# One more identity product for each node tile in three TensorE stages of a graph network kernel

## What is computed

```
x = x + L0_gnn(layernorm(x), ...)
x = x + L0_ffn(layernorm(x)[None], gate_w, gate_b, w1, b1, w2, b2, gamma, beta)[0]   # 16 experts, 2 chosen
x = x + L1_gnn(...)                                                                  # graph attention and a selective scan
x = x + L1_ffn(...)       # h = x @ W_gat (256 x 16), a_src and a_dst from it, 4 experts
x = x + L2_gnn(...)
x = x + L2_ffn(...)       # logits = x @ gate_w (256 x 8), 1 of 8 experts
x = x + L3_gnn(...)
x = x + L3_ffn(...)       # a router of two layers: relu(x @ router_w1) @ router_w2, 6 experts
```

## Time and profile before

| | |
|---|---|
| time, three executions | 5540.38, 5551.18 and 5554.88 us, median 5551.18 |
| span of the profiled execution (with the profiler on) | 6173.2 us; what lies around the span is not in the trace |
| PE busy | 4074.4 us, 66% |
| PEld busy | 2897.1 us, 47% |
| DVE, ACT, POOL busy | 3273.6, 2796.0 and 3072.9 us |
| mean granted TensorE clock | 0.802 of full speed |

### The profile page before, as it was taken

One profiled execution on the slowest core, in us unless ns is written; L12 is line 12 of the kernel. 1 busy time (PEld: TensorE's weight loads), 2 busy tenths in 40 slices (PEclk: granted clock), 3 DMA queues, 4 the chain that ended last, 5 costly groups with the idle time before them and its releaser, 6 DMA issues. The chain is left out here.

```text
span 6173.2 us, 66416 instructions
## 1 busy us (share of the span) xinstructions
PE 4074.4 (66%) x17366; PEld 2897.1 (47%) x17366; DVE 3273.6 (53%) x7095; ACT 2796.0 (45%) x6254; POOL 3072.9 (50%) x3130
## 2 busy tenths in 40 slices
PE   7888555567837777256485776857776774555665
PEld 4555333347824445222264444835555662223465
DVE  6444355456555566699634665255556125444532
ACT  4777333322335566466343442335553213666532
POOL 3666566633446566267414552436662323666333
PEclk8999777768957887699796887967776886777888
DMA  4444533355643333355502223543333324566356
GB/s 129 150 150 148 114 90 91 90 124 180 174 115 91 94 96 95 72 167 166 135 1 61 47 43 104 179 118 95 95 95 70 118 63 129 179 181 181 81 159 203
DMA packets 442553, 721.00 MB, mean 117 GB/s; under 512 B 150695, under 2 KB 322521, under 8 KB 437660
## 3 DMA queue, kind: packets, MB, share of 16 engines
q1 hardware_dynamic: 299057, 374.14, 21.6%
q0 software_dynamic: 139600, 337.72, 20.1%
q10 hardware_dynamic: 3530, 4.89, 0.2%
HBM read 565.71 MB, written 153.73 MB: 117 GB/s over the span
## 5 line engine op out<-in xcount | busy, mean ns | idle before, releaser
L631 PE MATMUL ps<-msg,same 128*125 128x256 f32 (+1 forms) x2496 | 953.6, 524 | 671.2 <-issue 269.6
L631 PEld LDWEIGHTS ps<-msg,same 128*125 128x125 f32 x2496 | 566.1, 251 | 986.6 <-issue 574.2
L888 POOL DMA_INDIRECT msg<-d_gat,src_i x416 | 406.0, 976 | 266.9 <-PE ps L949 137.8
L253 POOL DMA_INDIRECT rec<-rec,slot_i x391 | 379.7, 971 | 304.4 <-DVE rec L431 133.6
L607 POOL DMA_INDIRECT msg<-d_lin,src_i x416 | 393.2, 945 | 275.0 <-issue 101.9
L607 POOL DMA_INDIRECT msg<-rel_rows,src_rel x416 | 399.0, 959 | 223.1 <-issue 95.4
L607 POOL DMA_INDIRECT msg<-d_gat,src_i x416 | 393.5, 946 | 226.3 <-PE ps L631 90.7
L949 PE MATMUL ps<-msg,same 128*125 128x260 f32 x832 | 300.5, 495 | 175.9 <-DVE agg_c L1111 130.9
L278 PE MATMUL ps_f<-w,hs 128*128 128x256 f32 x1568 | 383.6, 398 | 48.9 <-DVE rec L431 30.4
L278 PEld LDWEIGHTS ps_f<-w,hs 128*128 128x128 f32 x1568 | 298.8, 196 | 156.9 <-issue 61.3
L2962 PE MATMUL ps_y<-pr,ident 128*128 128x447 f32 (+1 forms) x448 | 209.3, 593 | 238.3 <-DVE pr L3044 238.3
(11 more groups left out here) (632 smaller groups left out, 9885.5 us busy)
## 6 DMA issues: line engine op xcount, KB each, us to landing
w<-in_L_ffn_packed SPq DMA_DIRECT2D x170, 514.0 KB
fil<-rec SPq DMA_DIRECT2D x104, 512.0 KB
rows<-bc_d SPq DMA_DIRECT2D x96, 447.0 KB
rel_rows<-row SPq DMA_DIRECT2D x25, 896.0 KB
got<-answered SPq DMA_DIRECT2D x30, 560.0 KB
ahead<-in_L_ffn_packed SPq DMA_DIRECT2D x8, 2052.0 KB
lo_rows<-ffn_lo_r SPq DMA_DIRECT2D x32, 500.0 KB
msg<-d_gat,src_i POOLq DMA_INDIRECT x832
```

The lines of the kernel that those rows point to most:

```text
L253: nc.gpsimd.indirect_dma_start(k.rec, bass.IndirectOffsetOnAxis(slot_i[0:some_rows, c:c + 1], 0), rec[0:some_rows, g % R, j, :], None).the ...
L631: nc.tensor.matmul(ps[:, j, 0:width], same[:, g % 2, j, :], msg[:, g % R, j, 0:width], start=True, stop=True).then_inc(mm, 1)
L888: nc.gpsimd.indirect_dma_start(msg[:, g % R, j, :], None, table, bass.IndirectOffsetOnAxis(idx[:, n:n + 1], 0)).then_inc(msg_in[g % R], 16)
```

## The change

In the fronts without a router, and in the small head, TensorE does one more product for each tile: the identity as weights, the identity as moving operand, 128 columns, into a PSUM bank `ps_w` that nothing reads. It stands between the turning of a later tile and the narrow product of tile t. The product carries no wait and no semaphore. In the small head the bank comes from `ps_t`, which goes from four banks to three there, and the wait of `turn(t)` becomes one for the copy of tile t - 3. The wide heads and the front with a router keep their instructions.

```diff
@@ front
         else:
             w_sb = s.sb("w", [128, 2, L])
+            ps_w = s.ps("ps_w", [128, 128])
...
+                def keep_streaming():
+                    nc.tensor.matmul(ps_w[:], k.ident[:], k.ident[:], start=True, stop=True)
+
...
                     else:
+                        keep_streaming()
                         logits(t)
@@ head
-        ps_t, ps = s.ps("ps_t", [128, 4, 512]), s.ps("ps", [P, 4, 512])
+        narrow = width < 128
+        TURNED = 3 if narrow else 4
+        ps_t, ps = s.ps("ps_t", [128, TURNED, 512]), s.ps("ps", [P, 4, 512])
+        if narrow:
+            ps_w = s.ps("ps_w", [128, 128])
...
-                    if t >= 4:
-                        pe.wait_ge(copied, t - 3)
-                    nc.tensor.transpose(ps_t[:, t % 4, 0:P], rows[:, t, 0:128], k.ident[0:P, 0:P])
+                    if t >= TURNED:
+                        pe.wait_ge(copied, t - TURNED + 1)
+                    nc.tensor.transpose(ps_t[:, t % TURNED, 0:P], rows[:, t, 0:128], k.ident[0:P, 0:P])
...
                 for t in range(NT):
                     if t + 1 < NT:
                         turn(t + 1)
+                    if narrow:
+                        nc.tensor.matmul(ps_w[:], k.ident[:], k.ident[:], start=True, stop=True)
                     product(t)
```

More of the change, by code:

```diff
@@ L2326, in turn @@
                     pe.wait_ge(rows_done, t + 1)
-                    if t >= 4:
-                        pe.wait_ge(copied, t - 3)
-                    nc.tensor.transpose(ps_t[:, t % 4, 0:P], rows[:, t, 0:128], k.ident[0:P, 0:P])
-                    nc.tensor.transpose(ps_t[:, t % 4, P:2 * P], rows[:, t, 128:256], k.ident[0:P, 0:P]).then_inc(turned, 1)
+                    if t >= TURNED:
+                        pe.wait_ge(copied, t - TURNED + 1)
+                    nc.tensor.transpose(ps_t[:, t % TURNED, 0:P], rows[:, t, 0:128], k.ident[0:P, 0:P])
+                    nc.tensor.transpose(ps_t[:, t % TURNED, P:2 * P], rows[:, t, 128:256], k.ident[0:P, 0:P]).then_inc(turned, 1)
                 def product(t):
@@ L2356, in copy @@
                     act.wait_ge(turned, t + 1)
-                    nc.scalar.activation(cols[:, :, t * P:(t + 1) * P], ps_t[:, t % 4, 0:2 * P].rearrange("p (c n) -> p c n", c=2), ACT.Copy).then_inc(copied, 1)
+                    nc.scalar.activation(cols[:, :, t * P:(t + 1) * P], ps_t[:, t % TURNED, 0:2 * P].rearrange("p (c n) -> p c n", c=2), ACT.Copy).then_inc(copied, 1)
                 def keep(t):
```

## The result

The changed kernel takes 5577.78 us (median of five executions, 5574.15 to 5592.81) against 5549.69 us before (five, 5535.66 to 5554.88). The ratio is 1.0062 with a 95% interval of 1.0047 to 1.0077, so the change costs 26 to 43 us. The forecast was 5583.2 us.

What follows compares the result with a forecast made beforehand. The prediction took each of the three changed stages to be bound by TensorE at half clock; 75 added products at 0.43 us gave 32 us, so 5551.2 + 32.0 = 5583.2 us, with an eight-in-ten range of 5546 to 5596.

Steps and rivals of the forecast that it cites:

- The price of the product: Three changed stages: each added product costs two weight-load steps, 0.43 us at half clock, 0.22 at full.
- The sum of 32 us: All three changed stages: 75 added products at 0.43 us each, 10.7 us a stage.
- The bound from above: Added product priced as a two-matmul product that overlaps nothing: 0.59 us each, 44 us in all.
- The bound from below: Added product priced as two steps of the narrow products: 0.37 us each, 28 us in all.
- Nothing covers it: Three changed stages: TensorE's stream has no gap and DVE and ACT wait for it, so all 32 us show.
- The clock: Three changed stages: at 340 to 380 moving columns a us the clock stays at 0.50; chance 0.70.
- the bursts of 100 columns: Two bursts of 16 float32 matmuls, 428 columns a us within a burst, stayed at 0.50; used as comparison for the clock.
- A front rises in its opening: Rival: a front's dense opening, 490 columns a us, lifts the clock; one front saves 16.5 us, 5567 us; chance 0.12.
- If all three had risen: Rival: steady streams of all three stages reach clock 1.00, saving 17.4 us together, 5534 us; chance 0.13.
- The bank: Small head: losing one `ps_t` bank adds a wait that is always met; cost nothing.
- The queues: Stores and loads issue as before; DVE's rows wait for ACT's root, not TensorE; no cost of their own.
- From one execution to the median: The 32 us from the profiled execution is carried over unscaled to the unprofiled median of 5551.18 us.

Runs made afterwards that it cites:

- e2: Changed kernel with the added product cut to 16 moving columns from 128: 5577.99 us against 5544.13 for the kernel before, ratio 1.0058.
- e3: Changed kernel with two added products a tile in place of one, one behind the other: 5550.52 us against 5544.13 for the kernel before, ratio 1.0016.
- e5: Kernel before, no added product, narrow product widened with zero weights to 64 moving columns: 5549.28 us against 5544.02, ratio 1.0004.
- e9: Changed kernel with two added products a tile, the second between the two narrow products: 5589.49 us against 5540.27 for the kernel before, ratio 1.0088.
- e8: Kernel before plus float32 identity transposes ahead of the first turn (28 in fronts; 24 and 10 in small head), no product a tile: 5543.8 us, one execution.
- e6: Changed kernel plus identity products in the idle opening (14 in fronts; 12 and 5 in small head): 5523.02 us against 5544.02 for the kernel before, ratio 0.9953.
- e1: Kernel before with only the small head's turned-tile banks cut from four to three, no added products: 5553.8 us against 5544.1, one execution.
- e7: Kernel before plus identity products in the idle opening (14 in fronts; 12 and 5 in small head), none a tile: 5542.24 us against 5544.02, ratio 0.9991.

## Why the prediction was right, and where it was not

**The price of the product.** Two steps of 0.215 us, 0.43 us a tile, were forecast from the router front's rows; the changed front shows 0.43 and a tile of 1.587 us for 1.58. The sum of 32 us compares with 32.5 in the stretches. The bound from above, 0.59 us, was never near. The bound from below I had misread: a turn takes 0.46 us and not 0.42 (1348.16 to 1348.62), which leaves 0.35 us for two narrow steps, 26 us and not 28. What I had not said is whether the product's columns cost anything: e2 shows that they don't.

**Nothing covers it.** Right: all of it shows in the time, as the three stages are bound by TensorE at half clock.

**The clock.** The outcome was right: 0.50 in all three. The step behind it was only half right. That a stage can be busy throughout and not rise is borne out: the changed fronts are busy for 40.05 of 40.10 us and stay at half. But I compared means over a tile and leaned on the bursts of 100 columns as if they were a safe bound from above. The case was closer than I made it: with a second product the clock rises in the second front at 395 a us, 4% above the small head's 380 and below the bursts' 428. And the mean orders neither e3 against e5 nor e3 against e9. So the 0.50 was forecast with a measure that the runs don't bear out, and there was luck in it. Why the clock stays at half with one product and rises with two in a row is open.

The closing table of TensorE: Matmul & The Clock Gate, a page of the Trainium skill, advises to keep TensorE busy without a break for the full clock; this case does not agree, as the changed fronts have next to no break in 40 us and don't reach it, so the busy time that it speaks of must not be read off the profile's busy columns. Part 4 of the same page of the Trainium skill says that transposes don't count as other matmuls do; this case does not agree, as e8 shows a rise behind 28 of them.

**A front rises in its opening.** Not in the changed kernel's profile, where both fronts ran at half throughout; the four executions that were not profiled took 5574 to 5593 us, none near the 5567 of one rise. It did happen in e9, in one front of two (28.3 us where its twin takes 50.9), so the rival was real. Its price of 16.5 us for a front with one product a tile no run shows; nearest is e6, at full clock from the first turn, with 22.2 us where the changed front takes 40.1.

**If all three had risen.** e6 is nearest, as it has the change's tile at full clock: its streams are 22 us under before in all. I had said 17.4, with the first 3.5 us at half.

**The bank.** Right, nothing in the head's stream (e1).

**The queues.** Wrong, without weight for the time: I wrote that DVE's rows wait for ACT's root and not for TensorE. ACT's root stands in line behind its copies, and these wait for TensorE's turns. So a slower TensorE delays DVE's last group: the wait of 2.19 us became one of 6.00, and the group before it now waits 1.28 us. That is why DVE's last wait is 17.2 us and not the 22 I forecast: the 10.8 us of the front are shared among the three. It is off the path, as TensorE, busy for 40.05 of 40.10 us, still has scaled tiles to turn when it comes.

**From one execution to the median.** Carrying the term over unscaled was right: 32 forecast, 26 to 43 measured.

## What to carry to other kernels

A float32 product added to keep TensorE at full clock costs two steps a time, and where the clock doesn't rise it is pure loss; read off the granted clock of the stage, not its busy share, before and after. The time of a narrow float32 product hardly depends on its moving columns, so widen that operand first: with 96 or 128 columns a tile took 1.20 or 1.27 us at half clock, where 16 took 1.15, and the clock rose. What doesn't lift the clock may still hold it, so filling an idle opening and keeping a thin stream going belong together: the product alone cost 26 to 43 us, and the filled opening alone gained at most 11.

## What the runs showed of the hardware

- A float32 product with 16 moving columns costs as much as one with 128: 0.43 us at half clock, with two loads of 128 columns (e2).
- A stage can be busy for 50.86 of 50.90 us at half clock (e9), and with the same instructions in another order the clock rises after some 8 us (e3).
- A clock once at 1.00 holds there with one added product a tile, at 0.83 us a tile (e6), and falls within 5.4 to 11.1 us without it (e7).
- The clock rose behind 6.0 us and within 4.9 us of float32 transposes alone (e8).
